# Key stack copied group by group, values computed in three bursts and keys in four quarters of a loop body

## What is computed

```
def _L0_xattn_ref(query, key, value, ...):
    q = split_heads(query @ Wq.T + bq)          # 16 heads of 8
    k = split_heads(key @ Wk.T + bk)
    v = split_heads(value @ Wv.T + bv)
    scores = einsum('bhqd,bhkd->bhqk', q, k) / sqrt(8)
    out = einsum('bhqk,bhkd->bhqd', softmax(scores), v)
...
x = x + xattn(layernorm(x), ctx, ctx, ...)
x = x + attn(layernorm(x), ...)                 # a Mamba-2 block and a GELU MLP
x = x + ffn(layernorm(x), ...)                  # 8 experts, 2 chosen per token
```

## Time and profile before

| | |
|---|---|
| median of 3 runs | 583.64 us (582.66 to 584.8) |
| the profiled execution | 585.52 us, span 583.7 us |
| granted TensorE clock, mean | 0.97 |
| busy, share of the span | PE 90%, DVE 72%, ACT 65%, POOL 55% |
| DMA | 41.62 MB, of it k_stack 64 + 32 copies of 204 KB |

### The profile page before, as it was taken

One profiled execution on the slowest core, in us unless ns is written; L12 is line 12 of the kernel. 1 busy time (PEld: TensorE's weight loads), 2 busy tenths in 40 slices (PEclk: granted clock), 3 DMA queues, 4 the chain that ended last, 5 costly groups with the idle time before them and its releaser, 6 DMA issues. The chain is left out here.

```text
span 583.7 us, 18814 instructions
## 1 busy us (share of the span) xinstructions
PE 526.1 (90%) x7882; PEld 341.0 (58%) x7882; DVE 418.8 (72%) x749; ACT 380.7 (65%) x704; POOL 323.8 (55%) x197
## 2 busy tenths in 40 slices
PE   2887999999998897999999898999889888999997
PEld 1634555665565464655655565665457565777776
DVE  6187888798797695887887887735887578555554
ACT  4874667677678575776777776976582616656562
POOL 1697968558558456576577279602200024676673
PEclk9887999999999998999999998999999979999999
DMA  7898664674574571754752946101100000000001
GB/s 214 127 131 132 140 104 91 97 117 89 86 116 89 87 108 39 117 105 71 123 106 35 144 84 110 40 2 53 47 2 2 2 1 1 2 2 0 0 0 37
DMA packets 16425, 41.62 MB, mean 71 GB/s; under 512 B 4006, under 2 KB 6830, under 8 KB 16234
## 3 DMA queue, kind: packets, MB, share of 16 engines
q1 hardware_dynamic: 15608, 40.09, 39.6%
q10 hardware_dynamic: 740, 0.42, 0.2%
HBM read 19.70 MB, written 0.52 MB: 35 GB/s over the span
## 5 line engine op out<-in xcount | busy, mean ns | idle before, releaser
L899 DVE TENSOR_REDUCE half_max<-wide 128x2 f32<-128x802 f32 x256 | 241.8, 988 | 57.5 <-PE wide L584 53.6
L824 ACT ACTIVATE probs<-score 128x512 f32<-128x512 f32 (+1 forms) x416 | 225.8, 596 | 75.4 <-PE score L635 75.0
L655 PE MATMUL sums<-probs,values 128*32 128x192 f32 (+3 forms) x3328 | 134.7, 282 | 5.9 <-issue 5.9
L655 PEld LDWEIGHTS sums<-probs,values 128*32 128x32 f32 (+1 forms) x3328 | 87.8, 110 | 60.0 <-issue 31.6
L584 PE MATMUL wide<-k_stack,q_cur 48*128 48x401 bf16 x512 | 88.9, 343 | 13.3 <-ACT k_full L806 6.2
L635 PE MATMUL score<-q_cur,k_stack 50*128 50x128 bf16 (+1 forms) x1664 | 83.4, 219 | 9.6 <-ACT probs L824 5.0
L415 POOL TENSOR_TENSOR ctx_hi<-ctx_in,one 128x1601 bf16<-128x1601 f32 x15 | 42.9, 2860 | 77.3 <-PE wide L506 68.5
L635 PEld LDWEIGHTS score<-q_cur,k_stack 50*128 50x128 bf16 (+1 forms) x1664 | 52.3, 95 | 35.0 <-ACT probs L824 11.3
L1892 POOL TENSOR_TENSOR hid_lo<-hid_e,hid_hi 114x512 bf16<-114x512 f32 x47 | 54.2, 1158 | 32.7 <-ACT hid_hi L1916 31.4
L427 POOL TENSOR_TENSOR k_hi<-k_full,one 128x1601 bf16<-128x1601 f32 x15 | 42.9, 2857 | 43.2 <-ACT k_full L806 34.7
L2027 DVE SCALAR_TENSOR_TENSOR hid_e<-gu,keep_bgu,gate 114x512 f32<-114x512 f32 x48 | 35.9, 750 | 38.5 <-ACT gate L1929 38.3
(11 more groups left out here) (327 smaller groups left out, 923.7 us busy)
## 6 DMA issues: line engine op xcount, KB each, us to landing
k_stack<-k_hi SPq DMA_DIRECT2D x64, 204.0 KB, 6.5
ctx_in<-in_ctx SPq DMA_DIRECT2D x56, 200.1 KB, 3.2
k_stack<-k_lo SPq DMA_DIRECT2D x32, 204.0 KB, 8.7
ctx_in<-in_wgu SPq DMA_DIRECT2D x16, 171.0 KB, 4.9
keep_w<-in_w SPq DMA_DIRECT2D x1, 1368.0 KB
ctx_in<-in_ctx SPq DMA_DIRECT2D x1, 800.5 KB, 8.3
keep_x<-in_x SPq DMA_DIRECT2D x1, 512.0 KB, 6.9
q_cur<-shift SPq DMA_DIRECT2D x30, 2.0 KB
```

The source lines that it names most:

```text
L655: last = pe.matmul(sums[32 * g:32 * g + 32, first * LQ:(first + heads) * LQ], values[0:m, n, k, VW * g + 2 * c:VW * g + 2 * c + 32], probs ...
L824: nc.scalar.activation(probs[0:m, step % NPROB, :].rearrange("r (g p c) -> r p g c", g=G, p=2)[:, p], score[0:m, (2 * step + p) % NSCORE, ...
L899: dve.tensor_reduce(half_max[:, b % 2, :, u // 4, u % 4], wide[:, w, :].rearrange("p (c k) -> p c k", c=2)[:, :, 0:CH], AX.X, ALU.max).the ...
```

## The change

- The stack of a batch is copied group by group: for each group 6 DMAs of 16 rows (51 KB), 24 for a batch. Group 0 goes at step 0, the others at steps 2, 5 and 7 (`G_STEPS`). Each slot has a semaphore for each group, and the maxima wait for the group they read. For batch 0 all high parts go first, then the low ones.
- The values are made in three bursts of 5, 4 and 4 blocks at steps 1, 3 and 5.
- The keys are made in four quarters of one chunk at steps 6, 7, 8 and 10 (at 5, 7, 9 and 11 in body 0), each in a half of its own and with a copy of its own.

The amount of arithmetic and the bytes copied stay the same. The ring has 24 items in a body in place of 21.

```diff
--- before.py
+++ after.py
@@ -31,8 +31,9 @@
 PREFETCH = 3
 LEAD = 5
 M_LOW, M_SIGN, M_FIRST = 2, 3, 4
-V_STEPS, K_STEPS = (2, 5), (6, 8)
-H_STEP, L_STEP, C_STEPS = 1, 3, (8, 9, 11, 12)
+V_STEPS, K_STEPS = (1, 3, 5), (6, 7, 8, 10)
+V_FIRST = (0, 5, 9, 13)
+G_STEPS, C_STEPS = (0, 2, 5, 7), (8, 9, 11, 12)
 TAIL = 10
 NSPARE = 4
 
@@ -66,7 +67,7 @@
 
 def keys_at(i, k):
 
-    steps = K_STEPS if i else (9, 11)
+    steps = K_STEPS if i else (5, 7, 9, 11)
     return [(i + PREFETCH, steps.index(k))] if k in steps and i + PREFETCH < B else []
 
 
@@ -100,13 +101,13 @@
 def ring_order():
 
     order = [("k", 0, 0), ("k", 0, 1), ("x", 0, 0), ("q", 0, 0)]
-    order += [("m", 0, u) for u in range(16)] + [("t", 0, 0), ("v", 2, 0), ("v", 2, 1)]
+    order += [("m", 0, u) for u in range(16)] + [("t", 0, 0), ("v", 2, 0), ("v", 2, 1), ("v", 2, 2)]
     for i in range(B):
         for k in range(NK):
             order += [("m",) + unit for unit in units_at(i, k)[:1]]
             if k in V_STEPS and 0 < i < B - 2:
                 order += [("v", i + 2, V_STEPS.index(k))]
-            order += [("k",) + half for half in keys_at(i, k)]
+            order += [("k",) + quarter for quarter in keys_at(i, k)]
             order += [("m",) + unit for unit in units_at(i, k)[1:]]
             if k == turn_step(i) and i + 1 < B:
                 order += [("t", i + 1, 0)]
...
@@ -276,9 +277,9 @@
         def spare_emptied(e, what):
             e.wait_ge(s_spare_out, SPARE[what] + 1)
 
-        def stacks_of(b):
-
-            return s_stack[b % NSLOT], N_STACK * (b // NSLOT + 1)
+        def stack_lies(e, b, g):
+
+            e.wait_ge(s_stack[b % NSLOT][g], N_STACK * (b // NSLOT + 1))
 
         @block.sync
         def _(sp):
@@ -313,28 +314,34 @@
                     rows = slice(32 * r, 32 * r + 32)
                     sp.dma_start(ctx_in[rows, b % 2, :], A["ctx"][rows, b, :]).then_inc(s_ctx[b % 2], 16)
 
+            def stack_piece(n, g, term, keys):
+
+                for half in HALVES:
+                    at = half + PAIR * term
+                    sp.dma_start(k_stack[at:at + PAIR, n, g, :], keys[half + g:half + 64:G, :]).then_inc(s_stack[n][g], 16)
+
             def stack(i, b):
-                n, done = b % NSLOT, s_stack[b % NSLOT]
+                n = b % NSLOT
                 if b >= NSLOT:
                     sp.wait_ge(s_score, 2 * NK * (b - NSLOT + 1))
                 if b == 0:
                     sp.wait_ge(s_khi0, 2)
-                else:
-                    sp.wait_ge(s_khi, b)
-                for t in range(2):
-                    if t:
-                        at_step(i, H_STEP)
-                    for half in HALVES:
-                        at = half + PAIR * t
-                        sp.dma_start(k_stack[at:at + PAIR, n, :, :], k_hi[half:half + 64, :]).then_inc(done, 16)
-                at_step(i, L_STEP)
-                if b == 0:
+                    for g in range(G):
+                        for term in range(2):
+                            stack_piece(n, g, term, k_hi)
                     sp.wait_ge(s_klo0, 2)
-                else:
-                    sp.wait_ge(s_klo, b)
-                for half in HALVES:
-                    at = half + PAIR * 2
-                    sp.dma_start(k_stack[at:at + PAIR, n, :, :], k_lo[half:half + 64, :]).then_inc(done, 16)
+                    for g in range(G):
+                        stack_piece(n, g, 2, k_lo)
+                    return
+                sp.wait_ge(s_khi, b)
+                for g in range(G):
+                    if g:
+                        at_step(i, G_STEPS[g])
+                    for term in range(2):
+                        stack_piece(n, g, term, k_hi)
+                    if g == 0:
+                        sp.wait_ge(s_klo, b)
+                    stack_piece(n, g, 2, k_lo)
 
             def put_shift(b):
 
@@ -408,7 +415,7 @@
                     if b == 3:
                         spare_made(pool, ("k", 1, 3))
                 else:
-                    made = [RING["v", b - 2, 1]] + ([RING["k", b - 2, 1]] if b > 4 else [])
+                    made = [RING["v", b - 2, 2]] + ([RING["k", b - 2, 3]] if b > 4 else [])
                     if b == 4:
                         spare_made(pool, ("k", 2, 3))
                     pool.wait_ge(s_wide, 1 + max(made))
@@ -422,8 +429,9 @@
                 if b < PREFETCH:
                     spare_emptied(pool, ("k", b, 3))
                 else:
-                    is_empty(pool, ("k", b, 1))
-                pool.wait_ge(*stacks_of(b - 1))
+                    is_empty(pool, ("k", b, 3))
+                for g in range(G):
+                    stack_lies(pool, b - 1, g)
                 pool.tensor_tensor(k_hi[:, 0:LK], k_full[:, 0:LK], one[:].to_broadcast([P, LK]),
                                    ALU.mult).then_inc(s_khi, 1)
                 pool.wait_ge(s_khi, b)
@@ -551,22 +559,27 @@
                                      start=True, stop=True)
                 last.then_inc(s_spare, 1)
 
-            def keys(b, half):
-                n, w = b % 2, half_free(pe, ("k", b, half))
-                if b == 0:
-                    pe.wait_ge(s_low0, half + 1)
-                elif half == 0:
-                    pe.wait_ge(s_split, b)
+            def first_keys(half):
+                w = half_free(pe, ("k", 0, half))
+                pe.wait_ge(s_low0, half + 1)
                 for c in range(2):
                     at = CH * (2 * half + c)
                     last = product3(wide[:, w, 512 * c:512 * c + CH], wkv_hi[:, 0, :], wkv_lo[:, 0, :],
-                                    ctx_hi[:, n, at:at + CH], ctx_lo[:, n, at:at + CH])
+                                    ctx_hi[:, 0, at:at + CH], ctx_lo[:, 0, at:at + CH])
                 last.then_inc(s_wide, 1)
 
-            def vals(b, half):
-                n, w = b % 2, half_free(pe, ("v", b, half))
-                for k in range(7 * half, 7 + 6 * half):
-                    at = P * (k - 7 * half)
+            def keys(b, quarter):
+                n, w = b % 2, half_free(pe, ("k", b, quarter))
+                if quarter == 0:
+                    pe.wait_ge(s_split, b)
+                at = CH * quarter
+                product3(wide[:, w, 0:CH], wkv_hi[:, 0, :], wkv_lo[:, 0, :],
+                         ctx_hi[:, n, at:at + CH], ctx_lo[:, n, at:at + CH]).then_inc(s_wide, 1)
+
+            def vals(b, part):
+                n, w = b % 2, half_free(pe, ("v", b, part))
+                for k in range(V_FIRST[part], V_FIRST[part + 1]):
+                    at = P * (k - V_FIRST[part])
                     ks = slice(k * P, k * P + P)
                     last = product3(wide[:, w, at:at + P], ctx_hi[:, n, ks], ctx_lo[:, n, ks],
                                     wkv_hi[:, 1, :], wkv_lo[:, 1, :])
@@ -576,8 +589,9 @@
 
                 g, part = u // 4, u % 4
                 n, w = b % NSLOT, half_free(pe, ("m", b, u))
+                if part == 0:
+                    stack_lies(pe, b, g)
                 if u == 0:
-                    pe.wait_ge(*stacks_of(b))
                     pe.wait_ge(s_qcur, 2 * (b + 1))
                 at = min(CH * part, LK - CH)
                 for p, half in enumerate(HALVES):
@@ -645,7 +659,7 @@
                     if b < 2:
                         spare_emptied(pe, ("v", b, 3))
                     else:
-                        is_empty(pe, ("v", b, 1))
+                        is_empty(pe, ("v", b, 2))
                     if b:
                         pe.wait_ge(s_sums, b)
                 pe.wait_ge(s_exp, 2 * (NK * b + k) + 2)
...
@@ -798,14 +812,12 @@
                 act.dma_start(q_cur[half + TERM:half + TERM + 2, 0].rearrange("p g h q -> p (g h q)"),
                               shift[8 * p:8 * p + 8, :]).then_inc(s_shin, 16)
 
-            def keys_out(b, half):
-                w = filled(act, ("k", b, half))
-                src = wide[:, w, :].rearrange("p (c k) -> p c k", c=2)[:, :, 0:CH]
-                if half == 0 and b > 1:
+            def keys_out(b, quarter):
+                w = filled(act, ("k", b, quarter))
+                if quarter == 0:
                     act.wait_ge(s_klo, b - 1)
-                nc.scalar.activation(k_full[:, 2 * CH * half:2 * CH * half + 2 * CH].rearrange(
-                    "p (c k) -> p c k", c=2), src, ACT.Identity,
-                    bias=keep.vecs[:, V_BK:V_BK + 1]).then_inc(s_by_act, 1)
+                nc.scalar.activation(k_full[:, CH * quarter:CH * quarter + CH], wide[:, w, 0:CH], ACT.Identity,
+                                     bias=keep.vecs[:, V_BK:V_BK + 1]).then_inc(s_by_act, 1)
 
             def sums_out(b):
                 act.wait_ge(s_pv, NK * (b + 1))
...
@@ -886,12 +898,13 @@
                     op0=ALU.add, op1=ALU.subtract)
             last.then_inc(s_by_dve, 1)
 
-            def vals_out(b, half):
-                w, nk = filled(dve, ("v", b, half)), 7 - half
```

(19 more changed lines are left out.)

10 lines of the change are left out of this document (5 added, 5 removed).

## The result

| | before | after |
|---|---|---|
| median of 4 runs each, in turn on one chip | 584.22 us (582.66 to 586.09) | 613.11 us (607.76 to 616.68) |
| ratio | | 1.0485, interval 1.0391 to 1.058: slower |
| profiled execution, span | 585.52, 583.7 us | 615.64, 613.8 us |
| granted TensorE clock, mean | 0.970 | 0.939 |

The forecast was 576.5 us, with a range to 584. The kernel is 5% slower. Where do 30.1 us of span come from? Body 0 starts at 58.04 in place of 51.77, +6.3. From there to the end of body 15 it is 21.5 us longer, 12.9 of them in bodies 12 to 14 (72.8 in place of 60.0), and behind the attention 2.3.

The account below looks back on a forecast made before the run. TensorE was taken as nearest the limit, with DVE and ACT close behind and stalls on late instruction code. 585.5 + 3.1 (steps) - 10.7 (stalls) - 0.5 (start) = 577.4, less half of 1.9: 576.5 us; range 571 to 584.

Parts of the forecast that it names:

- the issue price of a piece: SP's queue: 0.40 us to issue one copy, 9.6 for all 24, beside 1.35 + 1.6 of other work in 21.4 us.
- Small DMAs are dear: Rival: SP or the queue becomes the bound, deciding from about 0.77 us a DMA; near 588 us; chance 0.02.
- The start: First unit, begun at 26.89, would wait for group 0 alone: -0.5 us, between -2.5 and +1.
- up to 1 us late: Loads queued on SP behind group 3, for steps 8 and 9, would go out up to 1 us late.
- five steps and more after their issue: Groups are needed at units 0, 4, 8 and 12, with this lead, so the new waits cost nothing.
- 5 us to spare: Group 3, issued at step 7, would land 5 us before POOL makes the next high keys near 19.8 us.
- The steps: Values and keys at new places in a body: together +0.26 us a body, +3.1 us for 12 bodies.
- the values: Three bursts of values: +0.6 us a body, with +0.66 before step 3's scores and +0.21 at step 4's unit.
- the keys: Keys in quarters: -0.3 us a body, with -0.33 at step 9, -0.33 at step 8, two bursts costing 2 x 0.10.
- The stalls: TensorE idle on "issue", read as late instruction code held up by stack copies: 12.7 us together.
- the term of 10.7: Us regained of the 12.7 lost to stalls, by gaps in the copy queue; the ends are 0 and 12.7.
- the 0.95 us that the forecast took off for this: The profiled execution stood 1.9 us above the median of three runs; half of that was taken off.
- that rival: The steps gain: each body 0.4 us shorter in place of 0.26 longer, about 5 us in all; 571.5 us; chance 0.12.

## Why the prediction was wrong

**The step that failed is the issue price of a piece.** "A DMA whose rows form a single dimension took 0.40 us to issue", "all 24 take 9.6" and "it fits" took the price from loads of `in_ctx`. The row right above it, four copies of `k_stack<-k_hi` in 3.04 us, was the same kind of transfer, from one place in SBUF to another, and gave 0.76. I argued that it was dear for its pattern, four groups in a row. Taken one by one, three of those four issues took 0.59 to 0.67 us and one 1.03, and the median of all 64 before is 0.60: the right price stood in the trace. The pieces took 0.59 each, 0.63 with the gap: 15.1 us undisturbed, 16.9 in body 6 with its wait and one slow issue.

**The rival that was right was mispriced.** "Small DMAs are dear" had the mechanism but a chance of 0.02, a limit at 0.77 us and 588 us. The limit asked when SP would be busy all of a body. SP does not have all of it. It can start only when the high keys are made, it waits for the low ones, and the shift rows must land before the next scores. In body 6 this leaves, for no delay of TensorE, 16.90 - 0.80 - 1.49 = 14.6 us, so **the issue decides from 0.61 us a piece**, where the pieces took 16.10 / 24 = 0.67, a slow one included. In body 5, where the loads took 0.99 and not 2.12, the same working gives 0.68. Undisturbed pieces of 0.63 stand just at the limit, and each slow issue goes past it. Above that limit each body pays, a late body pays again in the clock, and bodies 12 to 14, with the experts' loads, pay 13 us. So the change, with 21.6 us of own work in a body, needs 23.3 on average (233.2 for ten).

**Which cost it was.** The 51 KB pieces were dear, but not in transfer: a piece landed after 2.2 us, and the queue's share of the DMA engines fell from 39.6% to 21.0%. What they cost is their issue, on one engine's queue. The Trainium skill ("DMA: Bandwidth & Descriptors", Bandwidth) calls transfers under 64 KB descriptor-dominated and advises to batch them. Its advice points the right way here, though the cost in this trace is another. Its 0.95 us is the time of one transfer of 64 KB from HBM, issued by GpSimd. The prediction added 24 of them up to 594; the copies here overlapped, as the landing of 2.2 us beside a pitch of 0.63 shows.

**The start**, predicted at -0.5 with +1 as the worst, was +6.3. The first unit was indeed 1.2 us earlier. What I had not costed is what stands behind the pieces on SP: eight context loads, 13.8 us later, in front of the shift rows. The run with whole first copies gives 5.2 of it back.

**Loads "up to 1 us late"** was wrong in size: the first load of a body left SP 12.3 us into body 3 before and 17.6 us into body 6 after, but nobody waited for it. Groups needed only "five steps and more after their issue" held for the units, which never waited for their group. The "5 us to spare" before POOL's next high keys were not there: POOL waited 50.5 us in 9 waits for the last pieces. I looked at who waits for the pieces and for the loads, and passed over the two shift DMAs behind them, which are the only ones with no lead.

**What held.** The steps: +0.26 a body predicted, +0.27 measured, and also its parts, +0.59 for the values (0.6) and -0.27 for the keys (-0.3). The rows of body 5, in the change:

```profile
178.15 0.34 PE L598 MATMUL wide<-k_stack,q_cur 48*128 48x401 bf16 x2
178.99 0.40 PE L649 MATMUL score<-q_cur,k_stack 50*128 50x128 bf16 x8 [0.51 <-ACT probs L836]
...
182.14 0.34 PE L598 MATMUL wide<-k_stack,q_cur 48*128 48x401 bf16 x2 [0.28 <-DVE values L908]
...
190.10 0.39 PE L649 MATMUL score<-q_cur,k_stack 50*128 50x128 bf16 x8
190.67 0.34 PE L598 MATMUL wide<-k_stack,q_cur 48*128 48x401 bf16 x2 [0.19 <-ACT k_full L819]
```

The scores of step 3 wait 0.57 from the unit's end (178.15 + 0.27), where 0.66 stood. The unit of step 4, at 182.14, waits for DVE's copy of the values as the prediction said. The unit of step 9 begins 0.34 after the scores' 0.23, where 0.35 stood, and a quarter's copy takes 596 ns, where 0.60 was taken. The stalls too: they went with the gaps in the queue, in the change, with the pieces alone and with the copies spread. With the copies spread ten bodies are 9.9 us shorter, against 10.7 predicted for bodies 3 to 13. That is against one profiled execution with many stalls: the medians differ by 1.1%, some 6 us, so for a typical run the term of 10.7 was too large, and the 0.95 us that the forecast took off for this too little. Had a piece cost 0.40, the shift rows would have been in time, and the forecast's sum would stand but for this; that is argued from these terms, not shown by a run.

**Two sums in the prediction do not come out.** Bodies 0.4 us shorter in place of 0.26 longer are worth 12 x 0.66 = 7.9 us, not "about 5", so that rival's time would be 568.6 and not 571.5. And the terms of the steps as listed add up to +0.28 and not +0.26. Neither bears on the miss.

## What to carry to other kernels

Before a copy is cut into pieces, multiply their number by the issue time of the same kind of transfer, source and target alike, and follow the issuing queue from the moment it may start to the first thing behind the pieces that someone waits for; the free time between these two is the budget, not the length of the loop. If long transfers hold up instruction code, spread them and keep them whole. And when a producer is moved to a later step, look for waits on the whole of what it makes, even where the trace of before shows none.
